# Cross-attention and routed experts on one core: GpSimd's scatters in twos between its long operations

## What is computed

```python
qp = elu(layernorm(x) @ Wq + bq) + 1
kp = elu(ctx @ Wk + bk) + 1;  v = ctx @ Wv + bv
# per head, over time t:  sums += k_t v_t^T;  out_t = q_t sums;  Z = cumsum(qp)
x = x + (out / Z) @ Wo + bo
h = layernorm(x)
sel = argmax(softmax(relu(h @ W1 + b1) @ W2 + b2))
x = x + h @ expert_W[sel] + expert_b[sel]
```

## Time and profile before

| | us |
|---|---|
| median of 3 runs | 1085.85 |
| lowest, highest | 1083.83, 1088.55 |
| the profiled execution | 1082.15 |
| its span in the profile | 1080.4 |

### The profile page before, as it was taken

One profiled execution on the slowest core, in us unless ns is written; L12 is line 12 of the kernel. 1 busy time (PEld: TensorE's weight loads), 2 busy tenths in 40 slices (PEclk: granted clock), 3 DMA queues, 4 the chain that ended last, 5 costly groups with the idle time before them and its releaser, 6 DMA issues.

```text
span 1080.4 us, 37750 instructions
## 1 busy us (share of the span) xinstructions
PE 1011.4 (94%) x15784; PEld 721.9 (67%) x15784; DVE 884.8 (82%) x1924; ACT 374.7 (35%) x581; POOL 669.2 (62%) x576
## 2 busy tenths in 40 slices
PE   5689999999999999999999999999999999998873
PEld 2356666676677777766777777667777776676653
DVE  5579888888898888889888888898879888998552
ACT  1333333344333333333333333433333334332210
POOL 4334555557666666676666666766666667655665
PEclk9889999999999999999999999999999999999887
DMA  5556444445555444554555445545544545441461
GB/s 180 134 163 217 120 113 105 119 133 168 127 160 163 133 116 153 159 168 126 161 163 138 128 139 156 168 127 161 163 135 115 156 155 149 109 130 41 139 215 42
DMA packets 90921, 152.52 MB, mean 141 GB/s; under 512 B 19326, under 2 KB 57857, under 8 KB 90625
## 3 DMA queue, kind: packets, MB, share of 16 engines
q1 hardware_dynamic: 67184, 107.03, 36.7%
q0 software_dynamic: 12672, 33.84, 8.6%
q10 hardware_dynamic: 10896, 9.25, 2.8%
HBM read 98.20 MB, written 36.13 MB: 124 GB/s over the span
## 4 chain that ended last, share of the span: by engine, by line
PE 81%; DVE 6%; DMA 4%; issue 4%; POOL 3%; ACT 1%; SPq 0%; DVEq 0%; POOLq 0%
PE b_a L1030 26%; PE b_b L1035 18%; PE b_s L1132 9%; PE b_s L1057 6%; PE b_b L1080 5%; PE b_b L1090 5%; PE b_s L1070 3%; PE b_a L1025 3%; PE b_s L1098 2%; PE b_s L1117 2%; PE b_b L1132 2%; DVE stage L734 1%; DMA scales<-rstd 1%; DMA scale<-scales 1%; DMA buckets<-row,place 1%
## 5 line engine op out<-in xcount | busy, mean ns | idle before, releaser
L734 DVE TENSOR_TENSOR stage<-b_s,causal 128x1024 f32<-128x1024 f32 x192 | 225.7, 1217 | 11.7 <-PE b_s L1070 6.7
L517 POOL DMA_INDIRECT out<-rows x116 | 140.6, 1212 | 36.5 <-issue 31.0
L510 POOL DMA_INDIRECT buckets<-row,place x128 | 141.3, 1104 | 34.3 <-issue 33.7
L1030 PE MATMUL b_a<-x_T,wq_sb 128*128 128x512 f32 x256 | 129.2, 629 | 12.6 <-POOL x_T L537 7.2
L1030 PE MATMUL b_a<-ctxT,wk_sb 128*128 128x512 f32 x256 | 121.4, 618 | 11.0 <-DMA bias_k<-in_L_xattn_bk 9.6
L1035 PE MATMUL b_b<-wo_sb,attT 128*128 128x256 f32 x512 | 120.1, 388 | 6.2 <-DVE attT L948 6.2
L526 POOL TENSOR_TENSOR onehots<-onehots,onehot 128x32 bf16<-128x32 bf16 x32 | 7.8, 244 | 186.3 <-DVE place L875 186.3
L1035 PE MATMUL b_b<-wv_sb,ctxT 128*128 128x256 f32 x512 | 118.9, 385 | 0.0
L553 POOL TENSOR_TENSOR x_res<-x_res,bias_o 128x1024 f32<-128x1024 f32 x32 | 106.1, 3315 | 20.6 <-DMA x_res<-in_x 20.3
L1132 PE MATMUL b_s<-we_sb,x3T 128*128 x464 | 112.4, 385 | 2.9 <-DVE rows L841 2.2
L602 ACT ACTIVATE ex<-b_a,bias_k 128x512 f32<-128x512 f32 x64 | 44.0, 687 | 201.0 <-PE b_a L1030 186.8
(11 more groups left out here) (134 smaller groups left out, 1816.0 us busy)
## 6 DMA issues: line engine op xcount, KB each, us to landing
x_in<-in_x SPq DMA_DIRECT2D x32, 512.0 KB, 4.3
ctxT<-in_ctx SPq DMA_DIRECT2D x32, 512.0 KB
x_T<-in_xT SPq DMA_DIRECT2D x32, 512.0 KB, 4.7
qsel<-qp SPq DMA_DIRECT2D x256, 64.0 KB, 2.4
x_res<-in_x SPq DMA_DIRECT2D x32, 512.0 KB
rows<-buckets SPq DMA_DIRECT2D x116, 130.0 KB
scale<-scales ACTq DMA_DIRECT2D x32, 256.0 KB, 4.8
stage<-buckets SPq DMA_DIRECT2D x20, 130.0 KB, 3.5
```

The costliest lines, as they stand in the source:

```text
L510: pool.indirect_dma_start(buckets, bass.IndirectOffsetOnAxis(place[:, slot(route), t:t + 1], 0), row[:, slot(route), t, :], None).then_inc ...
L517: pool.indirect_dma_start(out.rearrange("t p n -> (t p) n"), bass.IndirectOffsetOnAxis(rows_of(i)[:, TOKEN:TOKEN + 1].bitcast(U32), 0), ro ...
L734: dve.tensor_tensor(dst.rearrange("p g h s q -> p g (h s) q"), b_s[:, :, 256 * t:256 * t + 256].rearrange("p g (a q) -> p g a q", q=C), ca ...
L1030: last = pe.matmul(dst, w[:, k, P * h:P * h + P], rows[:, k, :], start=(k == 0), stop=(k == KC - 1))
```

## The change

GpSimd's program alone is changed, in the order of its instructions within a step. Of the four output scatters the first two go ahead of z times u, the other two stay behind it. Of the four row scatters two stay behind residual plus bias, and the other two go behind the powers of the first norm, at the end of the step. In step 34 the extra output scatters stand between the two pairs of row scatters. The number of instructions and transfers is the same, and no wait is added or taken away.

```diff
@@ -544,9 +544,10 @@
                 if attend:
+                    scatter(slots_of(j - 1)[0:2])
                     pool.wait_ge(s_zinv, n(attend, k=1))
                     pool.tensor_tensor(z[:, :], z[:, :], u[:, :], ALU.mult).then_inc(s_zprod, 1)
-                    scatter(slots_of(j - 1))
+                    scatter(slots_of(j - 1)[2:4])
                     if group_no(attend) == 0:
                         pool.wait_ge(s_wld, WEIGHTS)
                     pool.wait_ge(s_xr[slot(attend)], 16 * half(attend) + 16)
@@ -554,7 +555,7 @@
                 if route and j < STEPS - 2:
-                    scatter_rows(route)
+                    scatter_rows(route, range(2))
                 if attend:
                     scatter(extra_slots_of(j))
                 for group in measured_in(j):
@@ -568,6 +569,8 @@
                     if group_no(group) == 0:
                         pool.memset(qsel[:, 1, :, :, :], 0.0).then_inc(s_qzero, 1)
+                if route and j < STEPS - 2:
+                    scatter_rows(route, range(2, GT))
 
             schedule(step)
```

## The result

| | before | after |
|---|---|---|
| median, us | 1083.35 | 1096.48 |
| lowest, highest | 1080.28, 1088.55 | 1094.92, 1098.17 |
| runs | 6 | 6 |
| profiled execution | 1082.15 | 1097.11 |
| its span | 1080.4 | 1095.4 |

The medians differ by 13.1 us, the means by 12.4. The ratio of after to before is 1.0114, 95% interval 1.0088 to 1.0141: slower.

A forecast was written before the change was run, and what follows sets the result against it. TensorE, busy for 94% of the span, was taken as the bound, so moved scatters count only if it waits. Terms 3.5 + 4.9 - 0.2 = 8.2 us took the median from 1085.85 to about 1094, range 1088.5 to 1098.5.

The forecast's parts named there:

- both places: Steps 6 to 8 and step 34, where late row scatters were to make TensorE lose 3.5 and 4.9 us.
- its own signs: Prediction wrong if step 7's TensorE gaps stayed, steps 10 to 30 changed length, or the tail swallowed part of 4.9.
- Steps 6 to 8: Row addition waits for late row scatters, delaying VectorE up to vsel; TensorE loses 3.5 us in all, between 0.9 and 5.7.
- Step 9: From step 8 to 9 the row addition starts 3.65 us after the powers, against 2.03 needed; loss 0.
- Steps 10 to 34: Output scatters ahead of z times u, and row scatters behind powers in 10 to 30, cost TensorE nothing; 0.
- the covers: Steps 10 to 34: 1.6 to 0.5 us before VectorE's u; steps 10 to 30: 2.1 us before the row addition.
- The rival by the weight load's wait for vsel: Shorter kp ends TensorE's weight-load wait in 25 steps, -4.7 us; 1087.5 in all, not slower; chance 0.11.
- the 0.2 us that the sum took off for it: Start of step 34: shortened residual plus bias lets rows go some 0.8 us earlier, worth perhaps 0.2.
- the objection from x2T: Against gain from an earlier vsel: the matmul behind TensorE's sums waits for ScalarE's x2T, which vsel doesn't touch.
- Step 34: Last row scatter ends 4.9 us later behind the extra output scatters, nothing covers it; +4.9, between 4.7 and 6.5.
- no slack further on: Tail after step 34 is one chain of TensorE, VectorE, last row scatters and reading back, so all 4.9 us stay.
- Port: Steps 10 to 34: kp and z times u exclude each other; second kp falls from 1.97 to about 0.7 us; taken as 0.

The follow-up runs named there:

- e9_three_rows: Changed kernel with a third `row` buffer and a slot ring of 12 instead of 15; 1175.81 us against 1238.7 for the kernel before, ratio 0.9507.
- e4_early: Kernel before with only the row scatters of steps 5 to 9 split, two behind the powers; 1236.42 us against 1235.6, ratio 1.0007.
- b2_before_again: Kernel before, unedited, run once more with its profile on a slower chip; 1231.95 us in one execution.
- e11_late_all: Kernel before with all eight scatters in a row at the end of each of steps 10 to 30; 1311.43 us against 1236.06, ratio 1.0591.

## Why the prediction was right, and where not

The forecast was 1094 us from 1085.85 and slower by 8.2; measured are 1096.48 and 13.1 in the medians, 15.0 between the profiles. The direction and both places were right. The two places together came to 8.8 us, 5.4 and 3.35, where 3.5 and 4.9 were forecast: that the two sums are so near is in part luck, as one was taken too small and the other too large. The other 6.2 us between the profiles lie outside the two places, where the prediction had next to nothing, and no run shows that the change brought them; as the medians of six executions each differ by 13.1, a part of them is probably in every execution. By its own signs the prediction was wrong in two points: steps of 10 to 30 changed their length, and the tail swallowed part of the 4.9.

- **Steps 6 to 8: mechanism right, term mis-sized.** Forecast 3.5 between 0.9 and 5.7, measured 5.4. The scatter's end came as worked out. The landing took 2.5 to 3.1 us from there, where I had let it take 1.6 to 2.5, and I took the middle of that. The 1.6 was a single landing; it should have been the end of the range, not half of the estimate. The 2.5 was a misreading: the median of 3.5 us in the earlier trace rows is made of 29 transfers of SyncE, and the 128 row scatters have no landing on record. The page of before has 20 of them in one line:

```profile
stage<-buckets SPq DMA_DIRECT2D x20, 130.0 KB, 3.5
```

The upper bound of this term so came from transfers of another kind. GpSimd's output scatters, which are of the right kind, took 3.7 us from issue to landing in the median of the same trace; less a scatter's own 0.97 that is 2.7, within what was measured. By the Trainium skill (DMA: Bandwidth & Descriptors, on the anatomy of one DMA) an estimate of the landing was 2.3 us from issue, and of the loss 0 to 0.7 a step. The trace disagrees: 155.41 to 159.07 is 3.7 us, and the loss 1.6 to 2.2. TensorE's loss came in three gaps, where I had looked for one of about 1.2 us at the sums (0.93 in step 7). That the wait for the landing is the cause is shown by `e9_three_rows`.

- **Step 9: the cover was there, 1.7 us came another way.** No row addition waits there, as forecast. But the granted clock fell to 0.68 in the projection, 5.41 us instead of 3.72. The sum had no term for this; I had looked at the clock of before alone, where it was 1.00. Whether the change brought the fall is open: the kernel before has it too on another chip, and `e4_early` with its late row scatters has not.
- **Steps 10 to 34: forecast 0, measured +3.2.** No u, attT or row addition came late: the covers held (z times u ends at 418.23 and u starts at 418.90 in the step quoted above). The rival by the weight load's wait for vsel did not come true either. Residual plus bias did not get shorter, as I had said: 3.62 us in the middle steps where it was 3.63, so no run shows the 0.2 us that the sum took off for it. The step's first sums begin 15.59 us into it before and after, so the objection from x2T was right. The 0.15 us that a clean step gains comes from the last sums, which are stretched less. Against that stand 5.3 us of gaps at the sums over values in eight steps. They begin behind the scatters, not beside them, and one of the same kind stands in step 4, ahead of all scatters; whether the new order or chance put them into these eight steps was not settled, as the first chip had no experiment.
- **Step 34: mechanism right, a part swallowed.** The last row scatter ends 5.2 us later (4.9 forecast), the row addition waits 6.75 us ("some 6"), and TensorE's first turning is late by the same 5.2. I wrote "no slack further on"; there was some: the 0.95 us between the two halves of the turning, and 0.9 in the stretch behind. 3.35 of the 5.2 are left. The earlier trace rows show only the second half; the first, and the gap ahead of the second, stand in TensorE's timeline, which I had not put beside the chain.
- **Start.** 1.3 us lie ahead of the first moved instruction. No step of the prediction could hold them, and nothing had yet run in the new order. Step 4 alone is 2.0 us longer, 0.9 of them the gap just named.
- **Port.** By the Trainium skill (SBUF — State Buffer, on the shared port pair) a VectorE instruction with two inputs in SBUF and a GpSimd instruction that reads SBUF exclude each other. The trace agrees for kp: the second took 0.68 us beside scatters instead of 1.97 beside z times u, and VectorE's 27 us less are that. It was worth nothing, since TensorE didn't wait for it.

The largest effect of the change was in no rival: on the chips of the experiments it takes 2.7 us out of each middle step. Why those chips show gaps of TensorE beside four scatters, where the first shows a stretch of 0.13 us, is open, and so is whether it belongs to the chips or to something else that differed between the sessions. That the scatters slow the supply of TensorE's instructions fits the missing releaser and the even pattern of a few matmuls and 0.4 us, but is only argued; the gap in step 4 needs no scatter. For the same reason I can't say which version is best everywhere. On the slower chips those with twos in the middle are, at 0.951 to 0.956, with or without the third buffer. On a chip like the first only the change as a whole was measured.

## What to carry to other kernels

An instruction that is moved behind a wait takes its landing with it: put the whole path, wait, scatter, landing, into the sum, take the landing at its slow end and from transfers of the same kind, and ask whether a further buffer makes it free. Look at the granted clock of each stretch that got longer: a fall cost 1.5 to 1.7 us here. Before it is put down to the change, look for it in a second trace of the kernel before. And before a change of order is called a gain or a loss, time it on more than one chip: this one was +1.1% on one and -4.7% on another.

## What the runs showed of the hardware that was not expected

- While GpSimd issues indirect scatters in a row, TensorE's short matmuls are stretched or come in groups of one to six with gaps of 0.4 us and more (`b2_before_again`, `e11_late_all`). The mean middle step was 33.5 us with scatters in twos, 36.2 with fours, 39.9 with eight, on chips of one kind; on another chip four in a row cost 0.13 us a step.
- Neither half alone gave the gain: outputs in twos 36.5 and 37.4, rows in twos 35.3, both 33.5. In the two middle steps shown, 1.5 of the 2.6 us between them are the fall of the clock behind the gaps (0.95 over the step, 1.00 with twos).
- At the same output projection ahead of step 9 the clock fell to 0.68 in one execution of the kernel before (5.41 us) and not in another (3.72), with 1.6 us of idle in the step ahead in both.
- The same kernel took 1083 us on one chip and 1232 to 1239 on three others, with the granted clock at 0.981 and at 0.956 in the profiles: an estimate from these two clocks is that the clock explains some 28 us of the 149, the smaller part; TensorE's gaps in the middle steps, 2.9 us a step against 0.2, are a larger one.
